# Cross attention begins within the last self steps; batch 1's chain between the cross units

## What is computed

```python
def attention(x, ctx, Wq, Wkv, Wo, bo):        # 16 heads of 16 features, scale 64 ** -0.5
    q = x @ Wq
    k, v = jnp.split(ctx @ Wkv, 2, axis=-1)
    out = softmax(q @ k.T * SCALE) @ v          # for each head
    return out @ Wo + bo
...
x = attention(ln1(x), ln1(x), Wq1, Wkv1, Wo1, bo1) + x      # self attention
x = attention(ln2(x), context, Wq2, Wkv2, Wo2, bo2) + x     # cross attention
lin, gelu = jnp.split(ln3(x) @ Wff1 + bff1, 2, axis=-1)
x = (lin * gelu * sigmoid(1.702 * gelu)) @ Wff2 + bff2 + x
...
K, V = context @ Wk.T + bk, context @ Wv.T + bv
out = softmax((x @ Wq.T + bq) @ K.T / 16) @ V @ Wfc.T + bfc
return norm_w * rms_normalised(out + x)
```

## Time and profile before

| | us |
|---|---|
| median of 3 runs | 757.97 (756.35 to 758.42) |
| profiled execution | 755.59 |
| its span, first to last instruction | 753.8 |
| self attention's last weighing ends | 442.1 |
| first cross score (L999) | 472.51 |
| first feed-forward product (L1078) | 565.48 |
| busy: TensorE, VectorE, ScalarE, GpSimd | 667.8, 548.8, 497.9, 72.1 |

### The profile page before, as it was taken

One profiled execution on the slowest core, in us unless ns is written; L12 is line 12 of the kernel. 1 busy time (PEld: TensorE's weight loads), 2 busy tenths in 40 slices (PEclk: granted clock), 3 DMA queues, 4 the chain that ended last, 5 costly groups with the idle time before them and its releaser, 6 DMA issues.

```text
span 753.8 us, 11125 instructions
## 1 busy us (share of the span) xinstructions
PE 667.8 (89%) x4072; PEld 319.8 (42%) x4072; DVE 548.8 (73%) x963; ACT 497.9 (66%) x893; POOL 72.1 (10%) x85
## 2 busy tenths in 40 slices
PE   4989799999999999999999973989979999999981
PEld 2644122222222222222224341445437888888870
DVE  6678989999999999999991728455654954343367
ACT  2542299999999999999999740667665333233374
POOL 2071800000000000000000202300020110000004
PEclk9999699999999999999999997899968999999995
DMA  9448350202020110100000021121000000000003
GB/s 300 179 147 274 103 184 1 71 1 70 2 71 1 38 35 1 29 2 29 1 2 1 15 79 48 46 68 34 3 1 0 1 1 1 1 1 1 1 0 111
DMA packets 35113, 36.87 MB, mean 49 GB/s; under 512 B 6132, under 2 KB 28276, under 8 KB 34804
## 3 DMA queue, kind: packets, MB, share of 16 engines
q1 hardware_dynamic: 33904, 35.87, 14.9%
q0 software_dynamic: 1024, 0.24, 0.3%
q10 hardware_dynamic: 132, 0.07, 0.0%
HBM read 23.09 MB, written 12.74 MB: 48 GB/s over the span
## 4 chain that ended last, share of the span: by engine, by line
PE 69%; ACT 13%; DVE 11%; issue 5%; POOL 1%; DMA 0%; ACTq 0%; SPq 0%; DVEq 0%; POOLq 0%
PE ps L902 17%; PE ps L890 12%; ACT probs L1274 8%; PE ps L688 6%; PE ps L1078 4%; PE ps L1079 4%; PE ps L1080 4%; PE ps L863 3%; DVE mm L1525 2%; PE ps L674 2%; PE ps L721 2%; PE ps L1007 2%; PE ps L696 2%; PE ps L1094 2%; PE ps L1093 2%
## 5 line engine op out<-in xcount | busy, mean ns | idle before, releaser
L1274 ACT ACTIVATE probs<-ps,unfit 128x512 f32<-128x512 f32 x512 | 313.2, 692 | 30.2 <-PE ps L890 24.0
L1525 DVE TENSOR_REDUCE mm<-ps 128x2 f32<-128x1024 f32 x256 | 300.9, 1219 | 17.0 <-PE ps L721 9.7
L890 PE MATMUL ps<-stack 50*128 50x512 f16 x512 | 149.0, 388 | 10.6 <-ACT probs L1274 0.4
L902 PE MATMUL ps<-probs,v 128*32 128x512 f32 x1024 | 137.2, 608 | 2.7 <-ACT outT L1279 2.7
L890 PEld LDWEIGHTS ps<-stack 50*128 50x128 f16 x512 | 36.5, 93 | 189.6 <-ACT probs L1274 182.7
L721 PE MATMUL ps<-stack 48*128 48x512 f16 x512 | 107.8, 390 | 10.2 <-DVE mm L1525 5.2
L1387 ACT ACTIVATE early<-ps,cols 128x512 f32<-128x512 f32 x32 | 22.0, 687 | 90.7 <-PE ps L1080 90.7
L1791 DVE SCALAR_TENSOR_TENSOR hid<-ps,cols,early 128x512 f32<-128x512 f32 x32 | 24.0, 750 | 70.2 <-PE ps L1080 70.0
L602 POOL TENSOR_TENSOR x<-x,rows 128x1024 f32<-128x1024 f32 x12 | 28.1, 2354 | 485.5 <-DVE tok L1506 485.4
L1332 ACT ACTIVATE probs<-ps,unfit 96x512 f32<-96x512 f32 x64 | 42.2, 680 | 25.5 <-PE ps L999 25.2
L1078 PE MATMUL ps<-x_hi,wff_hi 128*128 128x512 f32 x128 | 52.2, 408 | 0.0
(11 more groups left out here) (164 smaller groups left out, 863.0 us busy)
## 6 DMA issues: line engine op xcount, KB each, us to landing
v_groups<-early SPq DMA_DIRECT2D x8, 512.0 KB, 3.5
stack<-q_parts SPq DMA_DIRECT2D x64, 64.0 KB, 2.0
v<-v_groups SPq DMA_DIRECT2D x8, 512.0 KB, 4.1
x<-in_x SPq DMA_DIRECT2D x4, 512.0 KB, 8.0
q_parts<-probs SPq DMA_DIRECT2D x8, 256.0 KB, 3.8
k_parts<-probs SPq DMA_DIRECT2D x8, 256.0 KB, 2.6
stack<-k_parts SPq DMA_DIRECT2D x16, 128.0 KB, 2.5
stack<-q_parts SPq DMA_DIRECT2D x64, 32.0 KB, 1.9
```

Source lines behind the costliest of these rows:

```text
L890: eng.matmul(ps[:, st_bank(n), :], stack[rows_of(tile, KROWS), SLOTS + slot, q, P * kc:P * kc + P], qs[rows_of(tile, KROWS), slot, half, q ...
L902: mm_ = eng.matmul(ps[32 * h:32 * h + 32, PV, :], v1[:, G % 2, kc, 32 * h:32 * h + 32], probs[:, k % 2, h, :], start=(kc == 0), stop=(kc = ...
L1274: eng.activation(probs[:, k % 2, HEADS[h], :], ps[:, st_bank(n), :], ACT.Exp, scale=unfit[:, 0:1]).then_inc(exp_done, 1)
L1525: eng.tensor_reduce(dst, ps[:, 2 * slot:2 * slot + 2, :], AX.X, ALU.max).then_inc(s_red, 1)
```

## The change

- The copies and `high` of batch 0's chain move from ScalarE to VectorE; the chain has 16 pieces, spread two to a step from k = 5 to k = 11.
- In the last two self steps TensorE makes the four score tiles of cross group 0, behind self attention two of group 1. SyncE loads q2 of groups 0 and 1 block by block for them.
- Batch 1's whole chain runs between cross units, at most two pieces behind each. A group has 4 units, two heads in each: two score tiles side by side, one exp of 96x1024. Score tiles for maxima run 6 units ahead.
- GpSimd adds bo2 only when all of LN2 is done, biases go two tiles at a time, and GpSimd splits the first feed-forward weight too, behind the second.
- The last weighing stands ahead of the first feed-forward chunk, the last transposition of outT behind it.

Cut to what matters here:

```diff
-        TAIL = (1, 1, 1, 1, 1, 2, 1, 2, 1, 2, 2, 2)
...
-        UNITS = 8
...
-        PIECES_1 = ((1, 0, 1, 0, 1, 0, 1, 0), (1, 0, 1, 0, 1, 0, 0, 0))
...
+        TAIL = (1, 2, 2, 2, 2, 2, 2, 2, 1, 0, 0, 0)
...
+        UNITS = 4
+        S2_LEAD = 6
+        FIRST_S2 = 14
+        PIECES = ((2, 2, 2, 2), (2, 2, 1, 1), (1, 1, 0, 0), (0, 0, 0, 0),
+                  (0, 0, 1, 1), (1, 1, 1, 1), (1, 1, 1, 1), (1, 0, 1, 0))
...
+        SETUPS = {(2, 3): 1, (3, 0): 1, (3, 1): 2, (3, 2): 1, (3, 3): 2, (4, 0): 1, (4, 1): 1}
...
+        FF_PIECES = (0, 0, 2, 2, 2, 2, 2, 2)
...
             half = PROJ_2 + 2 * NC
-            for u in range(PROJ_2, half):
-                store_parts(u)
-            parts_stored(eng, half)
-            for G in range(SLOTS - 1):
-                load_q2(G)
+            for blk in range(2):
+                for u in range(PROJ_2 + NC * blk, PROJ_2 + NC * blk + NC):
+                    store_parts(u)
+                parts_stored(eng, PROJ_2 + NC * blk + NC)
+                for G in range(2):
+                    load_q2(G, (blk,))
+            load_max_2(0)
+            load_q2(2)
             eng.wait_ge(st_full, 64 * GROUPS)
-            load_q2(SLOTS - 1)
-            load_max_2(0)
+            load_q2(3)
             load_max_2(1)
             for u in range(half, half + NC):
                 store_parts(u)
+            load_max_2(2)
             parts_stored(eng, half + NC)
-            for G in range(GROUPS):
-                if G + 4 < GROUPS:
-                    eng.wait_ge(st_full, 64 * GROUPS + UNITS * (G + 1))
-                    load_q2(G + 4, (0,))
-                if G == 0:
-                    for u in range(half + NC, len(PROJ)):
-                        store_parts(u)
-                if G + 2 < GROUPS:
-                    load_max_2(G + 2)
-                if G == 0:
-                    parts_stored(eng, len(PROJ))
-                if G + 4 < GROUPS:
-                    load_q2(G + 4, (1,))
+            for G in (4, 5):
+                eng.wait_ge(st_full, 64 * GROUPS + UNITS * (G - 3))
+                load_q2(G, (0,))
+            for u in range(half + NC, len(PROJ)):
+                store_parts(u)
+            parts_stored(eng, len(PROJ))
+            load_q2(4, (1,))
+            load_max_2(3)
+            load_q2(5, (1,))
+            eng.wait_ge(st_full, 64 * GROUPS + UNITS * 3)
+            load_q2(6)
+            load_max_2(4)
+            eng.wait_ge(st_full, 64 * GROUPS + UNITS * 4)
+            load_q2(7)
+            for G in range(5, GROUPS):
+                load_max_2(G)
...
+                if n == 1:
+                    eng.wait_ge(tok_ready, 2 * TILES)
+                for i in range(0, TILES, 2):
+                    eng.wait_ge(tok_ready, TILES * n + i + 2)
+                    xb = x[:, i:i + 2, :]
+                    eng.tensor_tensor(xb, xb, rows[:, row:row + 1, :].to_broadcast([P, 2, D]), ALU.add).then_inc(bias_added, 1)
...
+                    parts_stored(eng, len(PROJ))
+                    eng.wait_ge(st_full, 64 * GROUPS)
+                    for f in range(FC):
+                        lo, w, hi = (v[:, :, :, f, :] for v in (wff1_lo, wff1_v, wff1_hi))
+                        eng.tensor_copy(hi, w).then_inc(w1_hi, 1)
+                        eng.wait_ge(w1_hi, f + 1)
+                        eng.tensor_tensor(lo, w, hi.bitcast(F32), ALU.subtract).then_inc(w1_lo, 1)
...
-            def scores_t2(G, n):
-                b, (half, h) = G // GPB, divmod(n, HG)
-                if n == 0:
+            def scores_t2(G, d):
+                b, (half, q) = G // GPB, divmod(d, HP)
+                if d == 0:
                     eng.wait_ge(m2_in[G % 4], 16 * HT * (G // 4 + 1))
-                eng.wait_ge(exp_done, 64 * GROUPS + UNITS * G + n - 1)
-                tile, q = divmod(HEADS[h], HP)
-                eng.matmul(ps[0:CTXP, ST + h % 2, :], k2[rows_of(tile, KROWS), b, G % GPB, q, 0:CTXP],
-                           qs[rows_of(tile, KROWS), Q2_SLOT[G % 4], half, q, :], start=True, stop=True).then_inc(st_full, 1)
+                eng.wait_ge(exp_done, 64 * GROUPS + UNITS * G + d)
+                for tile in range(HT):
+                    mm_ = eng.matmul(ps[0:CTXP, ST + tile, :], k2[rows_of(tile, KROWS), b, G % GPB, q, 0:CTXP],
+                                     qs[rows_of(tile, KROWS), Q2_SLOT[G % 4], half, q, :], start=True, stop=True)
+                mm_.then_inc(st_full, 1)
...
-            def cross_unit(G, n):
-                if G < GROUPS:
-                    scores_t2(G, n)
-                if G + 2 < GROUPS and n % 2 == 0:
-                    scores_2(G + 2, n // 2)
-                if n == 0 and G >= 1:
-                    turn_out_2(G - 1, 0)
-                if n == 1 and G >= 1:
+            def cross_unit(G, d):
+                scores_t2(G, d)
+                ahead = UNITS * G + d + S2_LEAD
+                if ahead < UNITS * GROUPS:
+                    scores_2(*divmod(ahead, UNITS))
+                if d == 0 and G >= 1:
                     weigh_2(G - 1, 1)
-                if n == 2 and G + 1 < GROUPS:
-                    turn_max_2(G + 1)
-                if n == 5 and G >= 1:
+                if d == 1 and G >= 1:
                     turn_out_2(G - 1, 1)
-                if n == 5 and G < GROUPS:
+                if d == 2:
+                    if G + 1 < GROUPS:
+                        turn_max_2(G + 1)
                     weigh_2(G, 0)
-            after_self = chain(0, 1)
-            advance(after_self, AHEAD)
-            eng.wait_ge(w_in["k2"], 16 * RUNS * B * GPB)
-            for n, count in enumerate(FIRST_S2):
-                G, t = divmod(n, KC)
-                if t % 2 == 0:
-                    scores_2(G, t // 2)
-                if (G, t) == (1, 3):
-                    turn_max_2(0)
-                advance(after_self, count)
-            after_cross = chain(1, 0)
+                if d == 3:
+                    turn_out_2(G, 0)
...
+                    if G == LAST and k == FIRST_S2:
+                        eng.wait_ge(w_in["k2"], 16 * RUNS * B * GPB)
+                        turned_out(LAST, TURN_0)
+                    if G == LAST and k >= FIRST_S2:
+                        scores_2(0, 2 * (k - FIRST_S2))
+                        scores_2(0, 2 * (k - FIRST_S2) + 1)
+            weigh(LAST, 15)
+            turn_max_2(0)
+            turn_out(2 * GROUPS - 1, CHAIN)
+            scores_2(1, 0)
+            scores_2(1, 1)
+            after_self, after_cross = chain(0, 1), chain(1, 0)
...
-            for n in range(6):
-                cross_unit(GROUPS, n)
+                    advance(after_self if G < GPB else after_cross, PIECES[G][d])
...
-                if n + 2 < FC:
-                    w1_high(n + 2)
...
+            def turn_copy(phase, blk):
+                for c in range(NC):
+                    eng.wait_ge(turn_full, 2 * TURNS.index((phase, blk)) + c + 1)
+                    src = ps[:, turn_bank(phase, blk, c), :]
+                    if phase == ATT1:
+                        eng.tensor_copy(attT[blk % 2][:, c, :], src).then_inc(turn_done, 1)
+                    else:
+                        i = COL_LN + 4 * (LN1, LN2, LN3).index(phase)
+                        eng.tensor_scalar(xT[:, c, BLK * blk:BLK * blk + BLK], src, cols[:, i + c:i + c + 1],
+                                          cols[:, i + 2 + c:i + 3 + c], ALU.mult, ALU.add).then_inc(turn_done, 1)
+            def high(u):
+                eng.wait_ge(pj_full, u + 1)
+                eng.wait_ge(fit_done, fits_of(u))
+                eng.tensor_scalar(part(u)[:, 0, :], ps[:, proj_bank(u), 0:BLK], fit_of(u), None, ALU.mult).then_inc(hi_done, 1)
             def chain(n, b):
-                for _ in range(2):
+                alone = (n, b) == (0, 0)
+                for i in range(2):
+                    if alone:
+                        turn_copy(ATT1, i)
                     yield
                 for i in range(KC):
                     blk, t = divmod(KC * b + i, TPB)
@@ -1642,14 +1645,16 @@
                 for i in range(2):
                     if i > 0:
                         finish_norm()
+                    if alone:
+                        turn_copy(LN2, i)
                     yield
                     if n == 0:
                         for o in range(NC):
+                            if alone:
+                                high(u)
                             remainder(u)
                             u += 1
                             yield
```

More of the change, by code:

```diff
@@ L598, in _ @@
             for n, row in enumerate((ROW_BO1, ROW_BO2, ROW_BFF2)):
-                for blk in range(BLOCKS):
-                    eng.wait_ge(tok_ready, TPB * (BLOCKS * n + blk + 1))
-                    xb = x[:, TPB * blk:TPB * blk + TPB, :]
-                    eng.tensor_tensor(xb, xb, rows[:, row:row + 1, :].to_broadcast([P, TPB, D]), ALU.add).then_inc(bias_added, 1)
+                if n == 1:
```

(53 more changed lines are left out.)

136 lines of the change are left out of this document (41 added, 95 removed).

## The result

The changed kernel takes 761.66 us (median of 20 runs, 757.18 to 765.82), the kernel before 756.81 (20 runs). The ratio is 1.0059, 95% interval 1.0040 to 1.0077. The forecast was 753.9 and faster. The prediction was wrong: it had the gain of the gap and nearly all the waits right, and TensorE's clock wrong. One limit of what follows: the two profiled executions of the unedited changed kernel took 757.93 and 757.75 us and are among its faster ones, so no trace shows an execution near its median.

The account below looks back on a forecast made before the run. TensorE was taken as the limit in the self tail and cross attention, waiting between them on VectorE's reductions. Terms +11.2, -26.8, +11.1, -2.6 gave -7.1; with 3 added for unplanned waits, -4.1: from 757.97 to 753.9 us, range 744 to 763.

Parts of the forecast that it names:

- Term 1: Tail of self attention: waits in its steps and 2 us for a lowered clock make it 11.2 us longer.
- Step 5: Tail of self attention: the first wo waits for the copies of the second transposition, +1.1 us.
- step 8: Tail of self attention: wo 6 waits for tile 4's add, which stands behind block 0's norm, +1.8 us.
- step 10: Tail of self attention: the projection waits for VectorE's copy, which stands behind block 1's norm, +3.5 us.
- Term 2: Gap from the last self step to the first cross score: 3.6 us where it was 30.3, so -26.8.
- rival D: Start of cross attention: late q loads put the first cross score 8 us later, 762 us in all; chance 0.04.
- Term 3: Cross attention up to the feed-forward part: 82.5 us of work and 21.5 of waits and clock, +11.1 us.
- Term 4: Feed-forward part: begins at full clock, and the first weight's splitting moves to GpSimd, -2.6 us.
- Group 3's wait: Cross attention: group 3's maxima stand on SyncE's queue behind a store and four loads; wait 4.6 us, clock 3 more.
- Rival C: Cross attention: GpSimd holds up VectorE's split_max in four groups, some +4 us, 758 us in all; chance 0.12.
- Rival B: Behind step 10 and at group 3: 12 us at 1.2 GHz each, costing 12 instead of 5; 761 us; chance 0.18.
- Rival A: Self tail and cross attention: a third of 35 us of waits and low clock doesn't come, 746 us; chance 0.20.

Follow-up runs that it names:

- the filled run: The changed kernel with 44 idle TensorE products in 13 places, in its waits of over 1 us, waits and queues kept: 748.14 us, ratio 0.9908 to the kernel before.
- three together: The changed kernel with batch 0's copies back on ScalarE, group 3's maxima ahead on SyncE's queue, GpSimd's additions behind group 2's maxima, no fills: 755.23 us.
- the control: The changed kernel itself, unedited, run again beside other edits: 761.7 us, ratio 1.0057 to the kernel before.
- the run with three edits and 32 fills: The changed kernel with ScalarE copies for batch 0, group 3's maxima earlier, GpSimd's additions later, and 32 idle products in remaining waits: 741.63 us, ratio 0.9832.

## Why the prediction was wrong, step by step

- **Term 1, mis-sized by 2.6.** Step 5 waited 0.94 (forecast 1.1), step 8 1.99 (1.8), step 10 3.40 (3.5). The failed step is "I charge 4 us of work at half speed, +2". The stretch at 423.2 held 5.07 us of work, cost 2.5, and a second one at 447.0 to 450.6, in steps 14 and 15, 1.7 more. It stands beside waits of 0.90 for the reductions: those waits were forecast, their clock wasn't. Together that is 4.2 of clock for the 2 charged, most of the 2.6. VectorE's copies took 0.76 (1.52 for two; forecast 0.7).
- **Term 2, right**: 3.58 for 3.6. The q loads were in time, so rival D is out.
- **Term 3, mis-sized by 4.5.** TensorE was idle for 108.60 - 90.56 = 18.0 us; the forecast was 21.5 less the 3 for the clock, 18.5. Group 1's waits of 1.74, 1.10, 1.18 and 2.22 make 6.2, with 0.64 before block 3's transposition 6.9 (forecast 6.5); that the sum fits is partly luck, for the first was forecast at 2.3 and the fourth at 1.3. The stage's work took 90.6 us and not 82.5 + 3. The failed step is again the clock: only group 3 was charged, and three more stretches lie in this stage (453.8, 488.0 and the one from 559.6). 23.4 us of its work stand in lowered stretches, which is 11.7 for the 3 charged, 8.7 too little. The work itself was overpriced: less those 11.7 it is 78.9, 3.6 under the 82.5 of the sum, and that hid part of the miss. The exp took 1.11 us (forecast 1.2).
- **Term 4, mis-sized by 5.0.** "The last cross units keep TensorE busy, so it begins at full clock" is the step that failed. Between 554 and 564 it waited 1.16 and 0.23 us for exps, 0.77 for VectorE's normed tokens and 0.54 for nothing that the profile names, none of them long, and the clock was low from 559.6 to 570.2. So 4.97 us of feed-forward work ran at 1.2 GHz, where it was 3.6. That is 2.5 of the 5.0. The rest is not the clock: the 0.8 for the splitting on GpSimd didn't come: waits of 0.74, 1.10 and 0.59 in the first chunks replaced those of 0.74 and 0.87, 0.8 more instead of 0.8 less. And the last transposition of outT (0.60 us at 570.30), which the change moves behind the first chunk, was left out of the term. Some 0.3 us stay unexplained.
- **Group 3's wait** was right in size (4.58) and in cause, the store and the loads ahead of the maxima. The run with the maxima first adds what the prediction didn't say: only 1.2 us of it can be had by their order, since the tile behind the score waits for the same store.
- **Rival C** was a real mechanism, and held up TensorE at one place, by 1.47 us, not 4. At a second (516.66) a half took 1.29 us instead of 0.19, and TensorE didn't wait for it; the other splits kept 0.18 and 0.19.
- **Rival B named the right cause, and its time fits by luck.** Its point of decision was half met: TensorE was at full clock again 5 us after step 10's projections began, but not 5 us after group 3's first score (510.60; the stretch ended at 519.0). Its time, 761, is what was measured, but it has 12 us of clock at those two places, where the stretches of 423.2 and 508.4 cost 2.5 and 4.2; the other 12.5 came from four stretches that it doesn't have. I gave it 0.18, because I tied the clock to the two longest waits. There were six stretches, and only two behind a wait of over 3 us; the filled run shows that together they were the loss.
- The expectation that a filled fall of the clock would stay filled was wrong too: with two waits filled, and with single waits removed, the lowered stretches moved to other places. It took fills in 13 places to leave one stretch.
- Rival A speaks of 35 us of waits and low clock in terms 1 and 3; the terms have 32.7. Nothing hangs on it here.

Not settled: why single edits worth 1.2 to 3.4 us of waits each moved the median by 4.5 to 5.9, when three together gave 6.5. That each happens to avoid one more stretch fits, but one profile of each doesn't show it. The traces do show that the stretches lie elsewhere from one execution to the next without an edit before them. The runs with the maxima first, with the norm in steps and with GpSimd late change nothing ahead of the first cross score, and it came 61.0, 58.8 and 61.1 us behind the mark in them, 59.6 in the control: in all three a lowered stretch of 3.6 us stood between 417.0 and 421.4, and in the control none before 423. So differences of 1 or 2 us between single traces can be the clock's place alone. Why the kernel before kept the stretch at 472 with its waits filled is open as well.

## What to carry to other kernels

Where TensorE works between short waits, price the clock with the waits, and not only behind the longest: here four of the six lowered stretches, with 25 of the 38.5 us of work in them, stood among waits of 0.2 to 2.2 us. Filling a long idle gap with work that has to wait every few microseconds can turn a mostly idle stretch at the low clock, which costs little, into a busy one, which costs half its work. Where the waits can't be removed, products into an unread bank, each group cut shorter than its wait, can keep the clock: here 44 of them were worth 10 to 13 us.

## What the runs showed of the hardware

- A product of 128x256 in f32 took 0.44 us on TensorE in a row of them (16 in 7.07, two records for each), and 0.22 for a record.
- GpSimd's addition of 128x512 beside VectorE's split of the maxima stretched two instructions from 0.18 and 0.19 us to 0.65 and 1.19, and beside its splitting of the weight one from 0.19 to 1.29; VectorE's reductions out of PSUM at the same time kept 0.79. The Trainium skill, page "SBUF — State Buffer", section "SBUF: two separate sides", names an exclusive lock on ports that both share; the trace agrees for these three.
- In the run with three edits and 32 fills the granted clock was 1.00 from 397 to 590 us, though waits of 1.16 and 1.35 us stood unfilled in it, and fell to half from 593.0 to 596.6, behind waits of 1.10 and 0.59. In the kernel before with all its waits filled it fell once (471.8 to 478.8), behind waits of 0.2 to 0.6 us with fills of 0.65 and 0.70 between them.
